# A fused block on one core: GpSimd instead of ScalarE begins eight of the first sixteen strip transfers of the attention

## The chip, the cores and the metric

The kernel runs on one core of one Trainium2 chip. The metric is the device time of one launch in microseconds (us). Times of single instructions come from one profiled execution. Engines: TensorE (PE; PEld is its weight load), VectorE (DVE), ScalarE (ACT), GpSimd (POOL) and SyncE (SP). ACTq and SPq are the issues of transfers in those engines' queues.

## The reference

`x` has 8 x 512 tokens of width 128, all in fp32.

```
x = x + 0.5 * ffn(layernorm(x))
x = x + attention(layernorm(x))     # one head, 4096 fixed memory keys and values
x = x + 0.5 * ffn(layernorm(x))

ffn:        sigmoid gate, the best 2 of 8 experts of 176 hidden units (bf16, squared relu),
            plus a shared expert in fp32
attention:  q = h @ Wq.T + bq;  p = softmax(q @ keys.T / sqrt(128));  (p @ values) @ Wo.T + bo
```

## The kernel before, in words

The tokens are 8 groups of 512 (4 tiles of 128). The first FFN runs over the groups up to about 118 us, the attention to about 560 us, the second FFN behind it. Each engine runs a fixed order written out by hand; semaphores connect them.

The attention has 16 **units** (u): a group of queries against one half (2048) of the keys. A unit has 8 **half steps** (h): tile i = h // 2 of the four, half h % 2 of its keys. In a half step TensorE computes the scores of 128 queries and 1024 keys (`scores`, six matmuls of 512 columns, L1311 to L1313, an fp32 product in three parts), VectorE takes their maximum (`maximum`, L1061; after the second half `neg_max`, L1067), and ScalarE the exponentials (`exponentials`, L726 or L736).

The product with the values needs the exponentials transposed, keys on the partitions. For some tiles of a unit this is done by VectorE, which transposes squares of 32 x 32 (`transpose_squares`, L1056), and by transfers that bring whole strips of squares from partitions i*32 to partitions b*32, from the tile `E2` to the tile `probsT` (`move_strip`, L331). There are 4 x 4 strips (b, i). In unit 0 two tiles (0 and 1) go this way, and tiles 2 and 3 ("own" tiles) are transposed by TensorE (`transpose_pair`, L1331); in the middle units it is three and one. In unit 0 each strip transfer is 32 partitions by two rows of 2 KB, 128 KB in all. They begin when the transposed squares of tiles 0 and 1 are there (`squares_done`); SyncE begins b = 0 and 1, eight transfers, ScalarE b = 2 and 3, eight transfers. In later units SyncE begins all but a few.

The strips are then used in pairs of key chunks, eight pairs (`ring`) to a unit: `moved_high` (ScalarE, L708) rounds the moved part, `moved_low` (GpSimd, L513) takes the rest; `own_high` (ScalarE, L700) and `own_low` (VectorE, L1049) do the same for the part that TensorE transposed; `values` (TensorE, L1352 to L1354) multiplies. In unit 0 the pairs begin early: ScalarE does moved_high(0) in half step 6, own_high(0) and moved_high(1) in half step 7; TensorE does transpose_pair(0) at half step 8, transpose_pair(1) at 9 and values(0) at 10. transpose_pair(1) waits for own_low(0) (`p_lo_done`), since both use the same PSUM bank. Scores use three pairs of banks in turn: a score block waits for the exponential three blocks before it.

The first `moved_high` of a unit waits for all sixteen strips of that unit:

```
if ring % UP == 0:
    for k in range(len(BATCHES)):
        wait(act, moved[k], moves(k, ring // UP + 1))
```

The eight transfers of ScalarE stand in its order behind the second exponential of tile 2 (u = 0, h = 5) and ahead of the first exponential of tile 3 (h = 6). In unit 0 GpSimd has nothing to do between its last instruction of the first FFN and `moved_low(0)`.

Of the kernel before, what the change touches and what calls it, by code (L numbers as in the profile page):

```python
# [17 lines left out]
GROUPS = TILES // GT  # L18
# [6 lines left out]
SLOTS = PAIRS + 1  # L25
# [13 lines left out]
LAST = UNITS - 1  # L39
# [5 lines left out]
SQ = 32  # L45
QUADS = P // SQ
# [41 lines left out]
def macaron_kernel(nc: bass.Bass, x, wup, wdown, gate_w, expert_bias, shared_up, shared_down,  # L88
                   wq, bq, wo, bo, keys_values, out):
    with ExitStack() as ctx:  # L90
# [3 lines left out]
        def sem(name):  # L94
            return ctx.enter_context(nc.semaphore(name))
# [35 lines left out]
        E2 = sb("E2", [P, MOVED, QUADS, N], fp32)  # L131
# [96 lines left out]
        down_done = sem("down_done")  # L228
        yT_copied = sem("yT_copied")
        z_done = sem("z_done")  # L230
# [8 lines left out]
        probsT_done = sem("probsT_done")  # L239
        squares_done = sem("squares_done")  # L240
        moved = [sem(f"moved{k}") for k in range(len(BATCHES))]
        p_hi_done = sem("p_hi_done")
        p_lo_done = sem("p_lo_done")
        moved_hi_done = sem("moved_hi_done")
# [16 lines left out]
        def wait(eng, s, n):  # L261

            if not isinstance(n, int) or n > 0:
                eng.wait_ge(s, n)
# [50 lines left out]

        def moves(k, units):

            return 16 * QUADS * QUADS * (units if k == 0 else max(0, min(units, LAST) - 1))

        def squares_of(units):  # L320
            return 2 * sum(moved_tiles(w) for w in range(units))
# [1 line left out]
        def batch_of(i):  # L323
            return [k for k, (first, count) in enumerate(BATCHES) if first <= i < first + count][0]

        def move_strip(eng, u, k, b, i):

            first, count = BATCHES[k]
            target = probsT[b * SQ:(b + 1) * SQ, u % 2, :, :, :].rearrange(
                "p (t i) c q -> p i t (c q)", t=MOVED)[:, i, first:first + count, :]  # L330
            eng.dma_start(target, E2[i * SQ:(i + 1) * SQ, first:first + count, b, :]).then_inc(moved[k], 16)  # L331

        def pairs_until(H):

# [57 lines left out]
        def _(pool):  # L392
# [144 lines left out]
            for u in range(UNITS + 2):  # L537
                g = u // 2
                for h in range(HALVES):

                    ring = pair_at(u * HALVES + h + 4)
                    if ring is not None:
                        moved_low(ring)
                    if has_next_group(u, u % 4) and h == 0:
                        inverse_deviation(g + 1 + ATTENTION_LN)
                        normalize(g + 1 + ATTENTION_LN, g + 1)
                    if u < UNITS and u % 2 == 1 and h == 1:
                        add_bias(g)
                    if 2 <= u < LAST and h == ADD_HALF:
                        add_block(u - 2)  # L550
                    if u == LAST + 1 and h == 4:
                        add_block(LAST - 2)
                    if u == LAST - 1 and h == 1:
                        inverse_deviation(SECOND_LN)
                        normalize(SECOND_LN, 0)
                    if u == LAST - 1 and h == 5:
                        inverse_deviation(SECOND_LN + 1)
                    if u == LAST and h == 3:
                        normalize(SECOND_LN + 1, 1)
                    if u == LAST and h == 4:  # L560
                        inverse_deviation(SECOND_LN + 2)
                    if u == LAST + 1 and h == 4:
                        inverse_deviation(SECOND_LN + 3)
# [4 lines left out]
        def _(act):  # L568
# [133 lines left out]
            def moved_high(ring):  # L702

                if ring % UP == 0:
                    for k in range(len(BATCHES)):
                        wait(act, moved[k], moves(k, ring // UP + 1))
                wait(act, pv_done, 2 * (ring - HI_RING + 1))
                act.activation(moved_part(p_hi, ring), moved_pair(ring // UP, ring % UP), ACT.Copy  # L708
                               ).then_inc(moved_hi_done, 1)

            def exponentials(u, i, h):

                v = u % 4
                act.wait_ge(neg_max_done, u * GT + i + 1)
                source = score_pair(u, i, h)
                if u == 0 and i == 0 and h == 0:
                    act.wait_ge(shared_up_done, GROUPS)
                    act.wait_ge(up_done, GROUPS * SLOTS)
                    act.wait_ge(weighted, GROUPS * SLOTS)
                if i < MOVED and h == 0:  # L720
                    wait(act, moved[batch_of(i)], moves(batch_of(i), u))
                    if u == 1 and i == MOVED - 1:
                        act.wait_ge(kv_lo_done, KV)
                if i < moved_tiles(u):
                    strips = E2[:, i, :, :].rearrange("p b (c q) -> p c b q", q=SQ)
                    act.activation(  # L726
                        strips[:, 2 * h * QUADS:2 * (h + 1) * QUADS, :, :],
                        source.rearrange("p k (c b q) -> p (k c) b q", b=QUADS, q=SQ), ACT.Exp,
                        bias=neg_max[:, v, i:i + 1], accum_out=row_sum[:, v, i, h:h + 1]).then_inc(exp_done, 1)
                else:  # L730
                    if i == MOVED and h == 0:

                        wait(act, probsT_done, UP if u == 1 else (u - 1) * UP)
                        if u < 2:
                            act.wait_ge(ffn_w_cast, 2)
                    act.activation(  # L736
                        own_exponentials(u, i)[:, 2 * h * N:2 * (h + 1) * N],
                        source.rearrange("p b n -> p (b n)"), ACT.Exp,
                        bias=neg_max[:, v, i:i + 1], accum_out=row_sum[:, v, i, h:h + 1]).then_inc(exp_done, 1)
# [23 lines left out]
            for u in range(UNITS + 2):  # L763
                g = u // 2
                prepares = u % 2 == 1 and u < LAST
                for h in range(HALVES):
                    H = u * HALVES + h
                    w = projection_at(H + 3)
                    if w is not None:
                        copy_oT(w)  # L770
                    if u == LAST + 2 and h == LAG - 2:
                        copy_oT(LAST)
                    if u == LAST + 1 and h == 3:
                        early_copy(1, banks[:, 1, :])
                    if u == LAST + 1 and h == 5:
                        exp_logits(GROUPS + 1, early_logits(1))
                        early_copy(2, banks[:, 0, :])
                    if u == LAST + 1 and h == 7:
                        exp_logits(GROUPS + 2, early_logits(2))
                    if u == LAST + 2 and h == 3:  # L780
                        copy_wbc(GROUPS, banks[:, 2, :])

                    ring = pair_at(H + 3)
                    if ring is not None:
                        own_high(ring)
                    if u < UNITS:
                        exponentials(u, h // 2, h % 2)
                    if u == 0 and h == 5:
                        act.wait_ge(z_done, GROUPS)
                        act.wait_ge(down_done, GROUPS * SLOTS)  # L790
                        act.wait_ge(squares_done, squares_of(1))
                        for b in range(QUADS // 2, QUADS):
                            for i in range(QUADS):
                                move_strip(act, 0, 0, b, i)
                    if 0 < u < LAST and h == HALVES - 1:
                        wait(act, moved_lo_done, UP * (u - 1))
                        act.wait_ge(squares_done, squares_of(u) + 2 * MOVED)
                        for i in range(QUADS):
                            move_strip(act, u, 1, QUADS - 1, i)
                    if prepares and h == Q_HALF - 2:  # L800
                        copy_xT_for_q(g + 1, TB)
                    if prepares and h == Q_HALF - 1:
                        q_high(g + 1, TB)
                    if u == LAST and h == Q_HALF - 2:
                        early_copy(0, TB)
                    if u == LAST and h == Q_HALF - 1:
                        exp_logits(GROUPS, early_logits(0))
                    ring = pair_at(H + 4)
                    if ring is not None:
                        moved_high(ring)  # L810
                    w = projection_at(H + 2)
                    if w is not None:
                        copy_y(w)
                    if 2 <= u and u % 2 == 0 and h == 1:
                        shift_exponentials(g - 1)
# [668 lines left out]
```

## Time and profile before

| | us |
|---|---|
| median of 3 runs | 663.71 |
| lowest, highest | 662.4, 664.31 |
| the profiled execution, its time | 662.44 |
| its span, first to last instruction | 660.8 |
| TensorE busy in the span | 614.2 |
| VectorE, ScalarE, GpSimd busy | 524.5, 461.3, 390.0 |
| mean granted clock of TensorE | 0.984 of full |

All times of rows are us from the span's start. The span is 1.64 us shorter than the execution's own time. An engine's busy time counts its instructions, not its waits and not the issuing of transfers.

### The profile page before, as it was taken

To read this page: it belongs to the slowest core of one execution; us is meant where nothing else is said; L and a number is where in the kernel's file an instruction comes from. 1 tells how busy PE (TensorE), PEld (TensorE's weight loads), DVE (VectorE), ACT (ScalarE), POOL (GpSimd) and SP (SyncE) were. 2 spreads that over 40 slices of the span, in tenths; PEclk is the share of its full clock that TensorE was granted. 3 is DMA by queue.
4 is the path that set the end of the run, shared out by engine and by line. 5 is a ranking of instruction groups with operands and counts; after the bars stand their busy time and mean duration, and the time that the engine had idled before them with its cause. 6 is when DMAs were issued, how large, how long until landed. Compare 5 with 4: busy or idle time off the path is not lost.

```text
span 660.8 us, 9207 instructions
## 1 busy us (share of the span) xinstructions
PE 614.2 (93%) x2800; PEld 429.1 (65%) x2800; DVE 524.5 (79%) x943; ACT 461.3 (70%) x765; POOL 390.0 (59%) x427
## 2 busy tenths in 40 slices
PE   3899999669899999999999999999999988999997
PEld 2555434447677877777778777777777867645442
DVE  4788877758978888887797897887898957698785
ACT  3567888446668767777776777777776774668886
POOL 3876970025366867767687587696677786524000
PEclk9799999979999999999999999999999998999999
DMA  8012020052573553744735627437355350000000
GB/s 301 1 33 65 32 64 0 2 126 65 128 160 87 137 132 76 172 95 101 160 84 141 135 64 176 107 93 163 90 131 116 84 121 1 0 18 17 32 33 32
DMA packets 35555, 59.06 MB, mean 89 GB/s; under 512 B 8539, under 2 KB 9139, under 8 KB 35379
## 3 DMA queue, kind: packets, MB, share of 16 engines
q1 hardware_dynamic: 31891, 53.75, 33.4%
q10 hardware_dynamic: 3616, 4.73, 2.8%
q8 instruction: 23, 0.38, 0.3%
q14 instruction: 25, 0.20, 0.1%
HBM read 8.12 MB, written 2.10 MB: 15 GB/s over the span
## 4 chain that ended last, share of the span: by engine, by line
PE 67%; DVE 18%; issue 5%; ACT 5%; SPq 1%; POOL 1%; ACTq 1%; DMA 1%; DVEq 0%; POOLq 0%
PE banks L1311 7%; PE banks L1352 7%; PE banks L1353 7%; PE banks L1354 7%; PE banks L1313 7%; PE banks L1312 7%; PE banks L1331 5%; DVE bank_max L1061 4%; DVE E L1056 4%; PE banks L1195 4%; PE banks L1186 3%; PE banks L1202 3%; PE banks L1149 3%; DVE probsT L958 3%; PE banks L1362 2%
## 5 line engine op out<-in xcount | busy, mean ns | idle before, releaser
L513 POOL TENSOR_TENSOR p_lo<-probsT,p_hi 128x768 fp32r<-128x768 f32 (+1 forms) x128 | 226.8, 1775 | 161.9 <-ACT p_hi L708 161.1
L1061 DVE TENSOR_REDUCE bank_max<-banks 128x1 f32<-128x1024 f32 x128 | 156.1, 1220 | 34.8 <-PE banks L1313 33.7
L708 ACT ACTIVATE p_hi<-probsT 128x768 fp32r<-128x768 f32 (+1 forms) x128 | 104.5, 816 | 28.0 <-PE banks L1354 24.0
L1311 PE MATMUL banks<-kv_lo,q_parts 128*128 128x512 f32 x256 | 112.0, 437 | 6.9 <-ACT E L726 4.4
L958 DVE SCALAR_TENSOR_TENSOR probsT<-banks,E 128x1024 bf16<-128x1024 f32 x80 | 95.5, 1218 | 28.7 <-PE banks L1186 28.1
L1056 DVE STREAM_TRANSPOSE E<-E 128x1024 f32<-128x1024 f32 x92 | 113.5, 1234 | 1.7 <-ACT E L726 1.7
L726 ACT ACTIVATE E<-banks,neg_max 128x1024 f32<-128x1024 f32 x92 | 102.3, 1113 | 8.5 <-DVE neg_max L1067 5.3
L1352 PE MATMUL banks<-p_hi,kv_lo 128*128 128x512 f32 x256 | 108.1, 422 | 0.0
L615 ACT ACTIVATE probsT<-probsT 128x1024 bf16<-128x1024 bf16 x96 | 91.8, 981 | 18.7 <-DVE probsT L958 15.5
L1353 PE MATMUL banks<-p_lo,kv_hi 128*128 128x512 f32 x256 | 102.8, 401 | 0.0
L1354 PE MATMUL banks<-p_hi,kv_hi 128*128 128x512 f32 x256 | 102.6, 401 | 0.0
L1313 PE MATMUL banks<-kv_hi,q_parts 128*128 128x512 f32 x256 | 101.6, 397 | 0.0
L1312 PE MATMUL banks<-kv_hi,q_parts 128*128 128x512 f32 x256 | 101.5, 397 | 0.0
L700 ACT ACTIVATE p_hi<-banks 128x256 fp32r<-128x256 f32 (+1 forms) x128 | 52.3, 408 | 63.1 <-PE banks L1331 62.9
L1049 DVE TENSOR_TENSOR p_lo<-banks,p_hi 128x256 fp32r<-128x256 f32 (+1 forms) x128 | 56.1, 438 | 43.1 <-ACT p_hi L700 42.6
L1331 PE MATMUL banks<-ident,probs 128*128 128x128 f32 x272 | 53.5, 280 | 10.7 <-ACT probs L736 6.6
L1311 PEld LDWEIGHTS banks<-kv_lo,q_parts 128*128 128x128 f32 x256 | 48.6, 190 | 15.3 <-ACT E L726 5.8
L1331 PEld LDWEIGHTS banks<-ident,probs 128*128 128x128 f32 x272 | 36.9, 143 | 32.9 <-ACT probs L736 7.0
L1354 PEld LDWEIGHTS banks<-p_hi,kv_hi 128*128 128x128 f32 x256 | 48.4, 189 | 12.4
L1352 PEld LDWEIGHTS banks<-p_hi,kv_lo 128*128 128x128 f32 x256 | 48.5, 190 | 11.8 <-issue 1.7
L1353 PEld LDWEIGHTS banks<-p_lo,kv_hi 128*128 128x128 f32 x256 | 48.5, 190 | 11.7 <-issue 1.7
L1186 PE MATMUL banks<-E,wup_b 128*128 128x512 bf16 x176 | 53.6, 392 | 2.4 <-DVE q_parts L1018 1.1
(118 smaller groups left out, 886.3 us busy)
## 6 DMA issues: line engine op xcount, KB each, us to landing
probsT<-E SPq DMA_DIRECT2D x248, 128.0 KB, 2.4
probsT<-E SPq DMA_DIRECT2D x168, 64.0 KB, 2.0
E<-in_keys_values SPq DMA_DIRECT2D x8, 512.0 KB, 3.5
probsT<-E ACTq DMA_DIRECT2D x56, 64.0 KB, 2.3
out<-X SPq DMA_DIRECT2D x8, 256.0 KB, 2.0
X<-in_x SPq DMA_DIRECT2D x1, 1280.0 KB, 8.9
probsT<-E ACTq DMA_DIRECT2D x8, 128.0 KB, 4.1
X<-in_x SPq DMA_DIRECT2D x3, 256.0 KB, 5.1
```

What stands on the lines that cost most here:

```text
L513: pool.tensor_tensor(moved_part(p_lo, ring), moved_pair(ring // UP, ring % UP), moved_part(p_hi, ring).bitcast(fp32), ALU.subtract).then_i ...
L708: act.activation(moved_part(p_hi, ring), moved_pair(ring // UP, ring % UP), ACT.Copy).then_inc(moved_hi_done, 1)
L958: dve.scalar_tensor_tensor(hidden[:, k, :, :], up_banks[PAIR_BANK[k]], 0.0, spread.unsqueeze(1).to_broadcast([P, 2, N]), ALU.max, ALU.mult ...
L1056: dve.transpose(half, half).then_inc(squares_done, 1)
L1061: dve.tensor_reduce(bank_max[:, i % 2, h:h + 1], score_pair(u, i, h).rearrange("p b n -> p (b n)"), AX.X, ALU.max).then_inc(bank_max_done, 1)
L1311: pe.matmul(bank, qh, kl, start=True, stop=False)
L1312: pe.matmul(bank, ql, kh, start=False, stop=False)
L1313: pe.matmul(bank, qh, kh, start=False, stop=True).then_inc(scores_done, 1)
L1331: last = pe.transpose(TB[:, at_column:at_column + P], own_exponentials(w, t)[:, c * P:(c + 1) * P], ident[:, :])
L1352: pe.matmul(OB, vl, hi, start=(c == 0), stop=False)
L1353: pe.matmul(OB, vh, lo, start=False, stop=False)
L1354: pe.matmul(OB, vh, hi, start=False, stop=(c == KC - 1)).then_inc(pv_done, 1)
```

## The change

The eight transfers of unit 0 that ScalarE began (b = 2 and 3) are begun by GpSimd, at the same half step of its own order, behind the same waits. Each gets a semaphore of its own (`moved_first`) in place of the common one, so the common count of unit 0 is eight transfers instead of sixteen (`moves`). ScalarE waits for the eight new semaphores ahead of moved_high(0), and again ahead of the first exponential of tiles 0 and 1 of unit 1, which overwrite the source.

```diff
+        moved_first = [sem(f"moved_first{k}") for k in range(QUADS * QUADS // 2)]
...
         def moves(k, units):
-            return 16 * QUADS * QUADS * (units if k == 0 else max(0, min(units, LAST) - 1))
+            if k == 0:
+                return 16 * QUADS * QUADS * units - (8 * QUADS * QUADS if units else 0)
+            return 16 * QUADS * QUADS * max(0, min(units, LAST) - 1)
...
-        def move_strip(eng, u, k, b, i):
+        def move_strip(eng, u, k, b, i, done=None):
...
-            eng.dma_start(target, E2[i * SQ:(i + 1) * SQ, first:first + count, b, :]).then_inc(moved[k], 16)
+            eng.dma_start(target, E2[i * SQ:(i + 1) * SQ, first:first + count, b, :]).then_inc(done or moved[k], 16)
...
             for u in range(UNITS + 2):            # GpSimd's order
                 g = u // 2
                 for h in range(HALVES):
+                    if u == 0 and h == 5:
+                        pool.wait_ge(z_done, GROUPS)
+                        pool.wait_ge(down_done, GROUPS * SLOTS)
+                        pool.wait_ge(squares_done, squares_of(1))
+                        for b in range(QUADS // 2, QUADS):
+                            for i in range(QUADS):
+                                move_strip(pool, 0, 0, b, i, moved_first[(b - QUADS // 2) * QUADS + i])
...
                 if ring % UP == 0:                # ScalarE, moved_high
                     for k in range(len(BATCHES)):
                         wait(act, moved[k], moves(k, ring // UP + 1))
+                if ring == 0:
+                    for done in moved_first:
+                        act.wait_ge(done, 16)
...
+                if u == 1 and i < 2 and h == 0:   # ScalarE, exponentials
+                    for done in moved_first:
+                        act.wait_ge(done, 16)
...
-                    if u == 0 and h == 5:         # ScalarE's order
-                        act.wait_ge(z_done, GROUPS)
-                        act.wait_ge(down_done, GROUPS * SLOTS)
-                        act.wait_ge(squares_done, squares_of(1))
-                        for b in range(QUADS // 2, QUADS):
-                            for i in range(QUADS):
-                                move_strip(act, 0, 0, b, i)
```

## Rows read from the trace of the kernel before

**Rows 1.** The page, engines' busy time; then the windows view of the attention.

```profile
PE 614.2 (93%) x2800; PEld 429.1 (65%) x2800; DVE 524.5 (79%) x943; ACT 461.3 (70%) x765; POOL 390.0 (59%) x427
...
144.75:540.00 395.25, 386.16 (x1821) 302.31 (x1819) 327.98 (x533) 289.38 (x526) 279.40 (x217) 1.00 0.51 118
```

**Rows 2.** The chain that ended last, 128 to 146 us: start, us, what.

```profile
130.72 0.75 ACTq L331
...
137.86 1.20 ACTq L331
...
139.10 0.02 ACTq L735
...
139.16 1.21 ACT probs L736 x2
```

**Rows 3.** The timeline of ScalarE: start, us, instruction, idle before and its releaser.

```profile
142.07 0.63 ACT L708 ACTIVATE p_hi<-probsT 128x512 fp32r<-128x512 f32 x1 [1.70 <-DMA probsT<-E]
...
143.08 1.10 ACT L736 ACTIVATE probs<-banks,neg_max 128x1024 f32<-128x1024 f32 x1
```

**Rows 4.** The timeline of VectorE.

```profile
133.71 0.15 DVE L1067 TENSOR_REDUCE neg_max<-bank_max 128x1 f32<-128x2 f32 x1
...
143.21 0.69 DVE L1049 TENSOR_TENSOR p_lo<-banks,p_hi 128x512 fp32r<-128x512 f32 x1 [6.93 <-ACT p_hi L700]
144.14 1.22 DVE L1061 TENSOR_REDUCE bank_max<-banks 128x1 f32<-128x1024 f32 x1 [0.23 <-PE banks L1313]
```

**Rows 5.** The timeline of TensorE.

```profile
140.42 1.12 PE L1331 MATMUL banks<-ident,probs 128*128 128x128 f32 x4 [6.60 <-ACT probs L736]
...
141.77 0.63 PE L1312 MATMUL banks<-kv_hi,q_parts 128*128 128x512 f32 x1
142.19 0.63 PE L1313 MATMUL banks<-kv_hi,q_parts 128*128 128x512 f32 x1
...
143.96 1.01 PE L1331 MATMUL banks<-ident,probs 128*128 128x128 f32 x4
...
146.44 0.40 PE L1353 MATMUL banks<-p_lo,kv_hi 128*128 128x512 f32 x1
146.68 0.40 PE L1354 MATMUL banks<-p_hi,kv_hi 128*128 128x512 f32 x1
...
550.78 0.38 PE L1331 MATMUL banks<-ident,E 128*128 128x128 f32 x1 [1.90 <-DVE p_lo L1049]
```

**Rows 6.** Windows: busy PE, PEld, DVE, ACT, POOL; granted clock, DMA share, GB/s.

```profile
25.28:35.52 10.24, 9.49 (x29) 5.95 (x30) 6.55 (x11) 5.95 (x9) 9.63 (x21) 0.50 0.01 2
550.78:554.34 3.56, 3.56 (x11) 2.98 (x12) 3.42 (x7) 0.91 (x2) 3.48 (x5) 0.52 0.00 0
137.92:140.42 2.50, 0.00 (x0) 0.00 (x0) 0.00 (x0) 1.21 (x2) 0.00 (x0) 0.50 0.89 243
140.42:144.74 4.32, 4.32 (x15) 3.36 (x15) 1.29 (x2) 2.67 (x5) 1.28 (x1) 0.50 0.14 37
132.10:141.60 9.50, 2.90 (x13) 2.23 (x12) 3.75 (x12) 1.21 (x2) 0.00 (x0) 0.81 0.89 221
160.00:167.40 7.40, 7.25 (x33) 5.33 (x33) 6.35 (x9) 4.50 (x10) 2.57 (x2) 1.00 0.92 203
```

**Rows 7.** The strip transfers (L331), issue ns min/median/max; units 0 and 1.

```profile
L331 ACTq DMA_DIRECT2D probsT<-E x8: 750/1026/1200, 130.7 to 137.9; - x8
...
DMA to landing us min/median/max: 2.6/4.0/4.4
...
L331 SPq DMA_DIRECT2D probsT<-E x14: 585/597/607, 158.7 to 167.1; - x14
...
DMA to landing us min/median/max: 2.4/2.4/2.5
```

**Rows 8.** The timeline of GpSimd.

```profile
142.77 1.28 POOL L513 TENSOR_TENSOR p_lo<-probsT,p_hi 128x512 fp32r<-128x512 f32 x1 [43.43 <-ACT p_hi L708]
...
179.53 1.84 POOL L513 TENSOR_TENSOR p_lo<-probsT,p_hi 128x768 fp32r<-128x768 f32 x1 [5.64 <-ACT p_hi L708]
```

## The prediction

> **What bounds the kernel now.** I read the page first. TensorE is busy 614.2 of 660.8 us, and over the long attention stretch from 144.75 to 540 us it is busy 386.16 of 395.25 us at full clock [rows 1]. So after 144 us there is next to no slack behind which lost TensorE time could hide: what delays TensorE there delays the end by the same amount.
>
> The chain of work that ended last, read between 128 and 146 us, goes through ScalarE's transfer issues from 130.72 to 139.06 us, then an exponential, and reaches TensorE at 140.42 us [rows 2]. Taken alone that looks like 8.3 us that could be had. But a chain follows only the last releaser at each step. So I read ScalarE's own timeline: after the issues it does the exponential of tile 3, first half (139.16), and then stops again, 1.70 us, until the transfers have landed, and does the first moved_high at 142.07 [rows 3]. moved_high(0) needs all sixteen transfers, SyncE's eight and ScalarE's eight. The question is therefore not when ScalarE is free, but when the last of the sixteen has landed. I call that time T; it is 142.07 us now.
>
> **Who waits for what around T.** ScalarE's order in the code is: exponential of tile 3 first half, moved_high(0), own_high(0), exponential of tile 3 second half. The three behind the first follow T directly, the last of them at 143.08 [rows 3]. VectorE's p_lo (own_low) follows own_high(0), at 143.21, and ends at 143.90; TensorE's transpose_pair(1) waits for it and starts at 143.96 [rows 4, 5]. From there TensorE has work without a break. None of these steps is shortened by the change. So TensorE's restart after the head is T + 1.89 before and after.
>
> **Part 1, ScalarE no longer issues: nothing on the path.** The maximum of tile 3 is there at 133.86 (133.71 + 0.15) [rows 4]. With the eight issues gone, the exponential starts at about 133.9 instead of 139.16, and TensorE, which follows its start by 1.26 us (139.16 to 140.42) [rows 2], does transpose_pair(0) and the next six score matmuls from 135.2 to 137.1: some 0.5 us for the transposes and 6 x 0.24 = 1.4 us by the distance of starts at full clock (146.44 to 146.68) [rows 5]. Then it stands until T + 1.89. What is gained is work that lies 5.3 us earlier and that nobody waits for: before, the same matmuls ended just when transpose_pair(1) became ready anyway. VectorE's maximum of those scores stands behind own_low in its order, so it moves only from 144.14 to 143.9 [rows 4]. The stall moves from before the exponential to behind it. Gain: 0.
>
> **Part 2, when the transfers land.** While the sixteen transfers run, the DMA engines are busy 0.89 of the time at 221 GB/s over 9.5 us, 2.1 MB [rows 6]; ScalarE's issues take 1.03 us each where SyncE's issues of the next unit, alone, take 0.60 us at every one, and landing takes 4.0 us where it then takes 2.4 (medians) [rows 7]. Two queues together carry hardly more than SyncE alone (221 against 203 GB/s) [rows 6], so the issues are held up by the engines, not the engines by the issues. GpSimd in ScalarE's place pushes the same bytes through the same engines. No row shows a transfer issued by GpSimd. Bounds for its issue, p, from the nearest rows: below, SyncE's alone, 0.64 us from start to start (fourteen starts from 158.7 to 167.1), which gives T = 130.72 + 8 x 0.64 + 1.8 (2.4 to landing less the issue) = 137.6; above, an ordinary GpSimd instruction, 1.84 us [rows 8], which gives 130.72 + 8 x 1.84 + 1.8 = 147.3. I take p where the same transfers now have it, 1.03 us [rows 7], so T stays at 142.07; shift 0, bounds -4.4 and +5.2. GpSimd itself has stood idle for 43.43 us when it comes to its first p_lo at 142.77 [rows 8]; behind the new wait and the eight issues (done by 139 at p = 1.03) stands only that p_lo, which waits for moved_high(0) in any case, so the cover holds until p is 1.4.
>
> The Trainium skill speaks here against a gain: "DMA: Bandwidth & Descriptors", "Rules for kernel authors", says that spreading transfers over issuing engines saves only issue time since the same engines move them. The rates of rows 6 agree. Its "Latency and other measured facts" gives the GpSimd path a first byte after about 1 us against 0.6 us; by that T would be an estimated 0.4 us later and the sum 0.4 us longer.
>
> **Part 3, TensorE's clock: a cost.** Before, TensorE stood for 6.60 us up to 140.42 [rows 5]. The granted clock was 0.50 from 137.92 on, 1.2 instead of 2.4 GHz, and stayed there until 144.74, 4.32 us after TensorE had resumed [rows 6]. But those 4.32 us mostly lay *ahead of* 143.96, where TensorE was waiting for T anyway; only 0.78 us of it fell on bound work. After the change TensorE stands from 137.1 to 143.96, 6.9 us, so the same dip comes, but TensorE resumes straight into bound work. By the starts of successive score matmuls (141.77 to 142.19, 0.42 us, against 0.24) [rows 5] each us at half clock loses 1 - 0.24 / 0.42 = 0.43 us. Cost: (4.32 - 0.78) x 0.43 = 1.5 us. Bounds: another dip lasted 3.56 us after TensorE resumed behind a gap of 1.90 us, the first of the run 10.24 us [rows 5, 6]: 10.24 gives (10.24 - 0.78) x 0.43 = 4.1 us. Below, no dip at all: -0.3 us, a gain of what it costs now (0.78 x 0.43). I take 1.5, since the gap is as long as the one that was followed by 4.32.
>
> **Part 4, the waits.** ScalarE gets eight more waits ahead of moved_high(0), and sixteen in unit 1. A wait of its queue shows as 0.02 us, and 0.04 us lie between it and the exponential behind it (139.10 to 139.16) [rows 2]; eight are at most 0.5 us if all stand behind T, and nothing if the last transfer is the last one waited for. I take 0.1. Those of unit 1 lie beside TensorE's work: ScalarE has room there (289.38 of 395.25 us busy) [rows 1]. Their cost if that cover were gone: 1.0 us.
>
> **The sum** against the profiled execution: 0 + 0 + 1.5 + 0.1 = +1.6 us. Its span is 660.8 and its time 662.44, so 1.64 us lie around the span; after: 664.0. The median of the runs before is 663.71, 1.27 above that execution, so I predict 665.3 us. A measurement of this kernel can't tell a change within 0.3% (2.0 us) from none, and this one lies just inside.
>
> **Rivals.**
> *GpSimd's stream runs out of step and lands sooner (faster).* SyncE and ScalarE run through the same source rows in lockstep; SyncE alone makes 203 GB/s [rows 6], so two streams that do not meet could carry more than 221 together. With SyncE done by about 137 and GpSimd at p = 0.87, T = 130.72 + 7.0 + 1.8 = 139.5, 2.6 us early. The gap is then 4.3 us; if the clock holds, the sum is -2.6 - 0.3 + 0.1 = -2.8: 660.9 us. It decides from T below 140.3 with the clock kept, or below 138.5 without. Against it: the low clock at 550.78 came behind a gap of 1.90 us alone [rows 5, 6]. For it: the gap would be a third shorter than the one that is followed by 4.32 us of low clock now. Chance 0.19.
> *GpSimd's issue is the slow one (slower).* With p = 1.5, between the row I take and the row above, T = 130.72 + 12 + 1.8 = 144.5, +2.5 us, and with parts 3 and 4 +4.1: 667.8 us. It becomes slower than 0.3% from T = 142.4, p = 1.24. The same holds if only the first transfer starts late, by 0.3 us or more, since GpSimd has issued none before. Chance 0.28. The Trainium skill ("GPSIMD Engine Reference", "Instruction dispatch") puts about 6 us on the first call of freshly loaded GpSimd code; if the transfer code were such a case the estimate would be 671.4. No row here shows whether it is.
> *The ScalarE stall was the bound after all.* If moved_high(0) were ready as soon as ScalarE is, the whole 5.3 us would come off: 658.4. Against it stands the 1.70 us wait for the transfers behind the exponential [rows 3]; I give it 0.03, which is in the faster chance of 0.20.
> *Nothing moves.* T stays and the dip is shorter or placed so that it costs under 1 us: 663.7 to 664.7. Chance 0.10.
>
> **How the numbers follow.** The forecast holds 0.40: T within 1 us of now and a dip of about 4 us behind the restart, +0.6 to +2.6 around 665.3; its own range is 664.3 to 666.3, and it splits 0.26 within 0.3% and 0.14 slower. With the rivals: faster 0.20 (both faster rivals, less 0.02 for a late T that keeps the clock), within 0.3% 0.38, slower 0.42. Range: below, the faster rival's 660.9; above, T of the slow rival with a longer dip (p = 1.6, T = 145.3, +3.2 + 2.6 + 0.1 = 5.9): 669.6. The ends p = 0.64 and 1.84 lie outside.
>
> **What would show it.** Right: ScalarE's exponential of tile 3 starts near 133.9; its moved_high(0) still near 142, now behind a wait of some 7 us for a transfer; TensorE has six score matmuls before 137.2 and a gap of nearly 7 us to about 144; the clock is 0.50 for some 4 us behind it, and transposes and scores there are 0.42 us apart. Wrong: T earlier than 140.3 or later than 143; GpSimd issues far from 1.03 us apart; the clock at 1.00 behind the gap.

## The result, and the profile after

The changed kernel takes 665.18 us (median of 20 runs, 662.37 to 668.69), the kernel before 663.57 us (20 runs, 660.48 to 665.49). The ratio is 1.0037, 95% interval 1.0023 to 1.0051: slower by 0.37%, clear of no change. A second series, with its own runs of the kernel before, gave 1.0021 (1.0004 to 1.0037). The recorded ratio is not the quotient of the two medians: these are 1.6 us apart in both series, 0.24% and 0.25%. The profiled execution took 665.67 us, its span 664.0 us, 3.2 us over that of before. One execution of e11 took 1066.41 us at a mean granted clock of 0.689 and is left out of its median and its ratio in the table.

First the issues of the strip transfers of unit 0 in the changed kernel: count, issue in ns min/median/max, first and last start.

```profile
L334 SPq DMA_DIRECT2D probsT<-E x8: 588/933/1917, 130.1 to 138.1; - x8
L334 POOL DMA_DIRECT2D probsT<-E x8: 533/533/787, 130.7 to 134.7; - x8
...
  ACT p_hi L721: 6.9, 1
```

GpSimd begins its eight within 4.5 us, the first issue taking 0.79 us and the others 0.53 us each, faster than SyncE alone does it in the next unit [rows 7]. But now SyncE's last issues are stretched, up to 1.92 us, and the last line says that ScalarE's moved_high waited 6.9 us for the transfers. The chain that ended last, and the packets from 139.7 to 142 us by queue, say for whose transfers it waited:

```profile
136.16 1.92 SPq L334
138.08 0.04 issue
138.12 3.28 DMA probsT<-E
141.40 0.02 issue
141.42 0.63 ACT p_hi L721
```

```profile
q1 hardware_dynamic: 126, 0.19, 31.5%
```

SyncE's last transfer is begun at 138.12 and lands at 141.40; in the last stretch SyncE's queue (q1) alone moves packets. GpSimd's eight transfers are through by then, so T is now set by SyncE's stream. The timeline of ScalarE shows where the stall has gone:

```profile
133.29 1.11 ACT L752 ACTIVATE probs<-banks,neg_max 128x1024 f32<-128x1024 f32 x1 [2.12 <-DVE neg_max L1076]
134.30 0.19 ACT L752 ACTIVATION_READ_ACCUMULATOR probs<-banks,neg_max 128x1 f32 x1
141.42 0.63 ACT L721 ACTIVATE p_hi<-probsT 128x512 fp32r<-128x512 f32 x1 [6.93 <-DMA probsT<-E]
...
142.43 1.11 ACT L752 ACTIVATE probs<-banks,neg_max 128x1024 f32<-128x1024 f32 x1
```

The exponential of tile 3 starts at 133.29 instead of 139.16, and the moved_high behind it at 141.42. The head of this execution ran 0.63 us earlier up to the first issue (130.08 instead of 130.71), so against the first issue T is 11.34 us, where it was 11.36 [rows 2, 3]. TensorE:

```profile
134.55 0.66 PE L1340 MATMUL banks<-ident,probs 128*128 128x128 f32 x4 [1.35 <-ACT probs L752]
134.96 0.48 PE L1320 MATMUL banks<-kv_lo,q_parts 128*128 128x512 f32 x1
...
136.21 0.40 PE L1322 MATMUL banks<-kv_hi,q_parts 128*128 128x512 f32 x1
143.32 1.11 PE L1340 MATMUL banks<-ident,probs 128*128 128x128 f32 x4 [6.71 <-DVE p_lo L1058]
...
145.93 0.63 PE L1321 MATMUL banks<-kv_hi,q_parts 128*128 128x512 f32 x1
146.36 0.63 PE L1322 MATMUL banks<-kv_hi,q_parts 128*128 128x512 f32 x1
...
147.94 0.40 PE L1362 MATMUL banks<-p_lo,kv_hi 128*128 128x512 f32 x1
148.18 0.40 PE L1363 MATMUL banks<-p_hi,kv_hi 128*128 128x512 f32 x1
148.42 0.60 PE L1340 MATMUL banks<-ident,probs 128*128 128x128 f32 x4
```

transpose_pair(0) and the six score matmuls lie early, then comes a gap of 6.71 us, and transpose_pair(1) starts at 143.32, T + 1.90. From there to transpose_pair(2) (148.42) it takes 5.10 us. In the first trace of before it took 3.66 us, from 143.96 [rows 5] to this line:

```profile
147.62 0.60 PE L1331 MATMUL banks<-ident,probs 128*128 128x128 f32 x4
```

The matmuls between start 0.43 us apart up to 147 and 0.24 us behind that. The windows say why (columns as in [rows 6]):

```profile
131.30:140.80 9.50, 3.96 (x19) 2.63 (x17) 3.74 (x12) 1.21 (x2) 3.91 (x8) 0.98 0.89 222
136.60:140.41 3.81, 0.00 (x1) 0.00 (x0) 0.00 (x0) 0.00 (x0) 0.00 (x0) 1.00 0.94 272
140.41:143.32 2.91, 0.00 (x1) 0.01 (x1) 0.75 (x2) 1.90 (x3) 1.19 (x1) 0.50 0.04 9
143.32:147.24 3.92, 3.92 (x12) 3.24 (x13) 2.13 (x4) 3.04 (x7) 1.84 (x3) 0.50 0.00 0
147.24:151.60 4.36, 4.36 (x22) 3.54 (x21) 4.00 (x4) 2.21 (x4) 4.14 (x9) 1.00 0.00 0
```

The transfers move at 222 GB/s, as before (221). The granted clock falls to 0.50 within the gap and stays there for 3.92 us after TensorE has restarted; in all that time TensorE is busy. So of the 3.2 us between the two spans, 1.44 us (5.10 - 3.66) arise here. The head gives 0.63 back. Of the other 2.4 us nearly all, 2.2 us, arise around 199 us: there TensorE stands 2.22 us instead of 1.38, at a wait for the strips of unit 1, and a stretch at half clock follows. The traces below show both kernels with such a stretch and without, so it can't be counted for the change.

### The profile page after: what moved, and what is told of

Its sections match the earlier page's. It is cut to its first block, busy times and chain, and to the rows that moved or that the text cites. A ratio compares the mean times of both kernels' runs of the same rounds, so it can differ in the third digit from the quotient of the medians.

```text
span 664.0 us, 9219 instructions
## 1 busy us (share of the span) xinstructions
PE 615.4 (93%) x2800; PEld 429.8 (65%) x2800; DVE 524.3 (79%) x943; ACT 461.0 (69%) x765; POOL 394.8 (59%) x435
## 3 DMA queue, kind: packets, MB, share of 16 engines
q0 software_dynamic: 384, 1.05, 0.6%
## 4 chain that ended last, share of the span: by engine, by line
PE 63%; DVE 17%; issue 5%; SPq 5%; ACT 5%; POOL 2%; DMA 2%; DVEq 0%; ACTq 0%; POOLq 0%
PE banks L1320 7%; PE banks L1322 7%; PE banks L1321 7%; PE banks L1361 7%; PE banks L1362 7%; PE banks L1363 7%; SPq L334 5%; PE banks L1340 4%; PE banks L1204 4%; PE banks L1195 3%; PE banks L1211 3%; DVE E L1065 3%; DVE bank_max L1070 3%; PE banks L1158 3%; DVE probsT L967 3%
## 5 line engine op out<-in xcount | busy, mean ns | idle before, releaser
L1322 PEld LDWEIGHTS banks<-kv_hi,q_parts 128*128 128x128 f32 x256 | 48.6, 190 | 11.6
```

The source lines that it names most:

```text
L1322: pe.matmul(bank, qh, kh, start=False, stop=True).then_inc(scores_done, 1)
```

## The experiments

T, the start of moved_high(0), is given against the first strip issue, which takes out what the head does from execution to execution. "Pair 1 to 2" is the time from the start of transpose_pair(1) to that of transpose_pair(2), all TensorE-bound work. "Gap" is TensorE's stand near 198 us, and "dip" whether the granted clock falls to 0.50 behind it. Each row's first three values come from one trace; the ratio is to runs of the kernel before made beside it.

| kernel | T, us | pair 1 to 2, us | gap, us; dip | median, us | ratio, 95% interval |
|---|---|---|---|---|---|
| before | 11.36 | 3.66 | 1.38; no | 663.57 | |
| e5, before | 11.33 | 4.29 | 1.45; no | 662.83 (one run) | |
| e12, before | 11.43 | 4.29 | 1.77; yes | 664.32 (one run) | |
| changed | 11.34 | 5.10 | 2.22; yes | 665.18 | 1.0037 (1.0023 to 1.0051) |
| e6, changed | 11.52 | 5.09 | 1.46; no | 664.86 | 1.0021 (1.0004 to 1.0037) |
| e9, fewer waits | 11.81 | 4.96 | 1.87; yes | 664.16 | 1.0027 (1.0007 to 1.0047) |
| e1, filled | 11.71 | 3.33 | 1.95; yes | 664.54 | 1.0036 (1.0018 to 1.0054) |
| e7, filled | 11.76 | 3.33 | 2.47; yes | 664.16 | 1.0009 (0.9995 to 1.0024) |
| e2, SyncE all | 12.14 | 4.85 | 2.18; yes | 666.21 | 1.0058 (1.0042 to 1.0073) |
| e3, changed, order | 10.65 | 5.45 | 2.42; no | 664.51 | 1.0023 (1.0003 to 1.0044) |
| e11, e3 filled | 10.68 | 3.31 | 1.83; no | 663.94 | 1.0029 (1.0005 to 1.0052) |
| e4, before, order | 10.05 | 3.31 | 1.95; no | 661.23 | 0.9978 (0.9960 to 0.9995) |
| e10, the same | 10.27 | 3.31 | 2.29; yes | 660.31 | 0.9970 (0.9947 to 0.9993) |
| e8, e4 filled | 10.09 | 3.33 | 1.94; yes | 663.52 | 0.9989 (0.9966 to 1.0012) |

**e1 and e7: is it the clock?** The changed kernel, and on TensorE, in the gap:

```diff
+                        if ring == 1:
+                            for _ in range(24):
+                                pe.matmul(OB, kv_hi[:, 0, 0:P], q_hi[:, 0, :], start=True, stop=True)
                         transpose_pair(ring)
```

> The changed kernel, with 24 matmuls of 512 columns that nobody reads put on TensorE (into the empty output bank) ahead of transpose_pair(1), where it stands for 6.7 us; 24 x 0.234 = 5.6 us, so they end before T + 1.89. Clock theory: the granted clock stays 1.00 behind the gap, the transposes and scores there run 0.24 us apart, transpose_pair(2) follows transpose_pair(1) by 3.7 us instead of 5.1, and the time falls by 1.4 to 1.8 us against the changed kernel, to about that of the kernel before (0.997 to 1.001 of it). Rival, the loss comes from GpSimd's path or from the waits and not from the clock: the time stays 1.5 to 2.5 us above the kernel before (1.002 to 1.004).

TensorE in e1:

```profile
136.51 5.77 PE L1449 MATMUL banks<-q_parts,kv_hi 128*128 128x512 f32 x24
143.77 0.66 PE L1340 MATMUL banks<-ident,probs 128*128 128x128 f32 x4 [1.48 <-DVE p_lo L1058]
...
146.86 0.40 PE L1363 MATMUL banks<-p_hi,kv_hi 128*128 128x512 f32 x1
147.09 0.60 PE L1340 MATMUL banks<-ident,probs 128*128 128x128 f32 x4
```

and its window of the restart:

```profile
143.50:147.00 3.50, 3.23 (x16) 2.71 (x17) 3.31 (x5) 3.29 (x7) 1.77 (x3) 1.00 0.00 0
```

At the place itself the theory holds: with TensorE kept busy the clock stays 1.00 and pair 1 to 2 takes 3.33 us instead of 5.10. The median did not follow; at 1.0036 it lay where the changed kernel's had been, which is what the rival had foretold for the time. So both kernels were measured again, side by side.

> The changed kernel once more, on the same chip as its neighbours here, for a second trace and a ratio taken beside theirs. Expected: 1.002 to 1.005 of before; T 11.3 us behind the first issue within 0.3; 4.7 to 5.5 us from transpose_pair(1) to (2), where before has 3.7; around 198 us either outcome.

> The kernel with the 24 filling matmuls once more, beside the changed kernel on one chip. Its first trace had the dip in the head gone and 3.33 us from transpose_pair(1) to (2) instead of 5.10, but its median came out as the changed kernel's (1.0036). If the clock's 1.5 us was real and the first median was scatter: 0.997 to 0.999 of e6. If the filling costs what it saves (T later: it was 11.73 us behind the first issue instead of 11.35): within 0.1% of e6, and T above 11.6 again.

The changed kernel came at 1.0021, the filled one at 1.0009. That is 0.12% or 0.8 us in the direction and the range of the clock theory, but the intervals overlap. T was 11.76 us, above the 11.6 of the other reading, but e9 has 11.81 without any filling, so that is no sure cost of it. The clock's cost is shown in the traces, in the medians only suggested. The granted clock of every execution is on record, not only that of the profiled ones. Its mean is 0.987 over 82 executions of the kernel before, 0.986 over 32 of the changed one and 0.990 over 20 of the filled one (e1, e7). So the change does not lower the clock by more than before did; it moves the low stretch onto work that nothing hides. And the filling does raise the clock in the runs without a trace too, yet little of that comes back as time.

**e2: does it need GpSimd?** The kernel before; SyncE issues all strips of unit 0, ScalarE's block is taken out.

```diff
-                    for b in range(QUADS // 2 if u == 0 else QUADS - k):
+                    for b in range(QUADS - k):
...
-                    if u == 0 and h == 5:
-                        ...
-                                move_strip(act, 0, 0, b, i)
```

> The kernel before with all sixteen strip transfers of unit 0 begun by SyncE and none by ScalarE; GpSimd issues nothing, no wait is added. Clock theory: ScalarE is free early, as in the change, T comes from SyncE's issues alone, 16 x 0.64 + 1.8 us behind the first, 12.0 instead of 11.4 us, so +0.7 us, and the dip behind the restart costs its 1.5 us again: +2.2 us against before (1.003). Rival, it is GpSimd that costs: only +0.7 us (1.001).

Its issues and what they lead to:

```profile
L331 SPq DMA_DIRECT2D probsT<-E x16: 587/597/736, 130.7 to 140.4; - x16
...
  ACT p_hi L708: 7.7, 1
...
DMA to landing us min/median/max: 2.4/2.4/2.5
```

T came out at 12.14 us (12.0 expected), TensorE stood 7.51 us, and pair 1 to 2 took 4.85 us, though GpSimd issues nothing and no wait is added. So the loss behind the restart belongs to the early start of ScalarE and not to GpSimd. Against e5 and e12 that is +0.8 us of T and +0.6 us behind it, 1.4 us; against the first trace of before 2.0. The ratio is 1.0058, 3.8 us: more than either theory gave, and the larger of the two (+2.2) is the nearer. What the rest is stays open; the mean granted clock of all six executions is low, 0.981 to 0.983, so some of it may be low clock at other places.

**e3 and e4: what sets T?** Only the order of the source strips in one of the two streams:

```diff
                         for b in range(QUADS // 2, QUADS):
-                            for i in range(QUADS):
+                            for i in (2, 3, 0, 1):
                                 move_strip(pool, 0, 0, b, i, ...)     # e3; in e4 the same for ScalarE's
```

> The changed kernel with GpSimd's eight transfers in the order of source i = 2, 3, 0, 1 in place of 0, 1, 2, 3, so that SyncE and GpSimd read other partitions at the same time. If the rate of 221 GB/s is one of partitions met by both streams: more than 260 GB/s, T 1.5 to 3.5 us earlier against the first issue (11.3 us now), and the time 1.5 to 4 us below the changed kernel. If the rate is that of the sixteen DMA engines whatever they read: T within 0.4 us and the time within 0.1% of the changed kernel.

> The kernel before with ScalarE's eight transfers in the order of source i = 2, 3, 0, 1, one edit. If the rate hangs on both streams meeting at the same partitions: T 1.5 to 3.5 us earlier against the first issue (11.4 us now), ScalarE's issues under 0.9 us each, and the time 1.5 to 4 us below before (0.994 to 0.998). If it is the engines' own rate: no change (0.999 to 1.001).

The issues of e4, and its transfers' window:

```profile
L331 SPq DMA_DIRECT2D probsT<-E x8: 587/603/1379, 128.6 to 134.1; - x8
L331 ACTq DMA_DIRECT2D probsT<-E x8: 617/807/1110, 128.7 to 134.3; - x8
```

```profile
130.00:138.00 8.00, 3.17 (x15) 2.31 (x14) 3.75 (x12) 1.21 (x2) 0.00 (x0) 0.94 0.96 262
```

```profile
136.59 0.73 PE L1331 MATMUL banks<-ident,probs 128*128 128x128 f32 x4 [4.83 <-ACT probs L736]
140.59 0.65 PE L1331 MATMUL banks<-ident,probs 128*128 128x128 f32 x4 [0.71 <-DVE p_lo L1049]
```

The same bytes by the same two queues go at 262 GB/s instead of 221, ScalarE's issue falls from 1.03 to 0.81 us (medians), T comes 1.3 us earlier (1.5 to 3.5 were expected), and TensorE's gap shrinks from 6.6 to 4.83 us. At 0.9978 it is faster than both the kernel before and the changed one. So the 221 GB/s was no rate of the sixteen engines whatever they read; it depended on both streams reading the same partitions in step. That is shown for the order. That the partitions' ports are what is met was not tried by itself. The Trainium skill ("SBUF — State Buffer", "Door 1: The DMA port swizzle") says that partitions 0 to 63 and 64 to 127 reach separate halves of the 16 DMA ports. That fits the order of e4, but no run here separates it from another cause. In e3 T moves by 0.7 us only, which neither branch of its expectation foretold. A likely reason, not tried, is that GpSimd begins its transfers 0.53 us apart and SyncE 0.60 us and more, so that the two soon fall out of the step that the order was made for. Its pair 1 to 2 is long again (5.45), and the ratio, 1.0023, lies between the two of the changed kernel, 1.0021 and 1.0037.

**e8, e10, e11: better versions.**

> A version meant to beat both: the kernel before with ScalarE's eight transfers in the order 2, 3, 0, 1, and 16 unread matmuls (3.7 us) on TensorE ahead of transpose_pair(0), in its gap of 4.8 us. Clock theory: no dip in the head, nothing lost behind transpose_pair(1), and 0 to 1 us below e4's 0.9978, so 0.996 to 0.998 of before. If filling costs by itself, as e1's median suggests: 0.998 to 1.000.

> The order 2, 3, 0, 1 for ScalarE's transfers in the kernel before, a second time, since it is the best so far (0.9978) and its version with filling matmuls came out unclear (0.9989). Expected: 0.996 to 0.999 of before, T 10.1 us behind the first issue.

> The changed kernel with both cures: GpSimd's transfers in the order 2, 3, 0, 1 and 24 filling matmuls. The traces so far give T 10.66 in place of 11.4 us (-0.7), 3.33 in place of 3.66 to 4.29 us from transpose_pair(1) to (2) (-0.3 to -1.0), and the filling's own delay of T (+0.3): -0.7 to -1.4 us, 0.998 to 0.999 of before. With 24 matmuls ending near T + 1.9 when T is early, up to 0.7 us of that may be lost, then 1.000.

e10 repeats e4: 0.9970. Whether filling adds anything to it can't be told (e8, 0.9989, 0.9966 to 1.0012), and at this place it had nothing to win: in e4 and e10 the low clock ended before transpose_pair(1), and pair 1 to 2 took 3.31 us without filling. e11 missed its expectation: its trace is as foretold, T 10.68 and 3.31 us behind the restart, and still its ratio is 1.0029. Two of the four filled series (e1, e11) lie clearly above what their first 150 us promise. What the filling costs elsewhere stays open, and the traces can't settle it. From transpose_pair(2) to the end of the span they take 513.2 us (before) to 517.4 us (e7), and e10, without any filling, takes 517.3. The best kernel is the one before with one list changed, not the changed one.

**e9: the waits.**

```diff
-                if u == 1 and i < 2 and h == 0:
-                    for done in moved_first:
-                        act.wait_ge(done, 16)
```

> The changed kernel without the sixteen waits in unit 1 (moved_high(0) has waited for the same eight transfers already). My term for all added waits was 0.1 us, with those of unit 1 hidden. Expected: within 0.1% of the changed kernel (1.0021 of before beside its neighbours), and the times from transpose_pair(1) to (2) and on to unit 2 as they were. Rival, the waits cost what they would without cover: 1.0 us or 0.15% less than the changed kernel.

1.0027 against the changed kernel's 1.0021 and 1.0037: nothing gained. The intervals (0.2% to each side) don't rule out the 0.15% of the rival, but the traces speak against it: from transpose_pair(2) to the first moved_high of unit 1, behind these waits, e9 took 31.45 us, and the changed kernel 31.38 and 31.56 us with them.

**e5 and e12: the place near 198 us.**

> The kernel before once more, for a second trace. In the first traces the changed kernel loses time at two places: 1.44 us between transpose_pair(1) and (2), and 2.4 us around 198 us, where ScalarE waits for the strips of unit 1 (TensorE stands 2.2 us instead of 1.4, and a dip of the clock follows). If the second place comes from the change: here TensorE stands 1.2 to 1.5 us again and no dip follows. If it is chance from execution to execution: 1.4 to 2.4 us, with or without a dip. The 3.66 us from transpose_pair(1) to (2) should come again within 0.4 us in either case.

> The kernel before a third time, for the two places that differ from execution to execution. Expected: T 11.3 to 11.5 us behind the first issue, 3.3 to 4.3 us from transpose_pair(1) to (2). If the place around 198 us is chance: TensorE stands between 1.4 and 2.5 us there, as it did in the other traces; if the change moved it: 1.4 us again, without a dip behind it.

e5 left the question open, since a gap of 1.45 us without a dip fits both readings. It missed at the other place: transpose_pair(1) to (2) took 4.29 us, where 3.66 within 0.4 was expected. e12 took 4.29 us as well. In these two traces the low clock lasted 10.24 us and ended 2.1 us behind the start of transpose_pair(1), where in the first trace of before it ended 0.78 us behind it.

e12, the kernel before, at the place near 198 us:

```profile
193.00:199.50 6.50, 4.73 (x23) 3.60 (x22) 3.15 (x5) 2.82 (x5) 3.57 (x3) 1.00 0.67 158
199.75:203.16 3.41, 3.41 (x10) 2.66 (x9) 2.51 (x5) 2.09 (x4) 3.08 (x2) 0.50 0.41 97
```

The dip of 3.41 us at half clock is there in the kernel before too, while e6, the changed kernel, has neither the long gap nor the dip. So the 2.2 us at this place in the first pair of traces must not be counted for the change. They are part of the scatter of single runs, some 5 us. Whether the change makes such a dip more likely, fourteen traces can't tell.

## Why the prediction was right

- **The chain's 8.3 us of issues are no gain: right.** ScalarE's exponential moved from 139.16 to 133.29 and T did not. The stall moved behind it, 6.93 us in place of 1.70.
- **T stays, since the rate and not the issue holds it: right in the size, half right in the reason.** T went from 11.33 to 11.43 us (three traces) to 11.34, 11.52 and 11.81, about +0.2 us. But I took p as 1.03 us with 0.64 as the lower bound; it is 0.53 behind the first issue, below the bound. With p = 0.53 my bound's formula gives T = 130.72 + 4.2 + 1.8 = 136.8, 5.3 us early. It did not happen, because SyncE's issues became slower as GpSimd's became faster (up to 1.92 us), and SyncE's last transfer set T. The transfers together hold T, at 222 GB/s against 221, and the formula, which had only one stream's issue in it, does not. Why SyncE's stream is the one held back was not tried; the same 1.05 MB went as 384 packets in GpSimd's queue and as 640 in SyncE's. "The same engines carry the same bytes" was too strong as a reason: e4 shows that their rate depends on the order.
- **The clock: right.** Gap 6.9 foretold, 6.71 measured; low clock behind the restart 4.32 foretold, 3.92 measured; 0.42 us from start to start against 0.43; cost +1.5 us against +1.44 in the first pair of traces. That this pair agrees so well is partly luck. I took the 0.78 us of low clock on bound work from one trace; it was 2.1 us in e5 and e12. Over all traces the cost is less, since before varies (3.66, 4.29, 4.29) where the change hardly does (5.10, 5.09, 4.96): +1.0 us on the mean. e2 has it without GpSimd, e1 and e7 lose it with the clock kept up.
- **The waits: right**, too small to see. Those of unit 1 gained nothing when they were taken out (e9). Those ahead of moved_high(0) cost nothing either: only 0.02 us lie between the last landing, at 141.40, and its start at 141.42, so the 0.2 us of T are not theirs.
- **The sum:** 1.6 us foretold. The places add up to 1.0 + 0.2 = 1.2 us; the two series measured 2.5 us (0.37%) and 1.4 us (0.21%) by their ratios and 1.6 us each by their medians. The 1.2 us rest on three traces of each kernel, and what the first series' ratio has above them is not accounted for. The median of 665.18 lies 0.1 us beside the predicted 665.3, which is partly luck: 665.3 was built on 663.71, and the twenty runs before gave 663.57. By the bound of 0.3% the first series is just on the slower side, where I had 0.42, against 0.38 for within it.
- **The rivals.** GpSimd's stream did run out of step with SyncE's, and in stretches the rate was higher (272 GB/s from 136.6 to 140.4), but the whole did not land sooner: SyncE had been held back. The slow GpSimd issue did not come. GpSimd's first issue did start late, 0.6 us behind SyncE's, which is more than the 0.3 us that I gave as enough for "slower". It cost nothing, since GpSimd's eight transfers were through before SyncE's. The 6 us that the Trainium skill ("GPSIMD Engine Reference", "Instruction dispatch") puts on freshly loaded code did not come either: the first issue took 0.79 us. (My 671.4 for that case should read 671.3, 665.3 + 6.) The rule of the Trainium skill ("DMA: Bandwidth & Descriptors", "Rules for kernel authors") that spreading transfers over issuing engines saves only issue time agrees with T, 11.34 to 11.81 us against 11.33 to 11.43.

## What to carry to other kernels

A chain of waits that runs through an engine's transfer issues does not say that the time would come free with them: look at the next instruction that needs the transfers' *landing*, and at which stream's last transfer it waits for. Work that is brought forward into the shade of a wait can cost: here TensorE then stood 6.7 us directly ahead of bound work and restarted it at half clock, where before it spent most of the slow stretch on work that had time. And where two queues move data between partitions at once, try the order in which they walk through them first; here one list was worth 0.2 to 0.3%, where moving the issues to another engine cost 0.2 to 0.4%.

## What the runs showed of the hardware that I had not expected

- GpSimd issues these transfers (32 partitions, two rows of 2 KB each) faster than SyncE or ScalarE: 0.53 us apart, at most 0.79 for the first, against 0.60 for SyncE undisturbed. Its issues were not stretched while the DMA engines were loaded (median 0.533 us); SyncE's were, to 1.92 us.
- SyncE's and ScalarE's queues, reading the same partitions in step, made 221 GB/s; with one of them two strips ahead, 262 GB/s.
- Filling TensorE's gap with unread matmuls kept the granted clock at 1.00 behind it in all four traces, and yet the medians of e1, e7 and e11 did not fall by as much as their traces gained there. Not explained.
- The same kernel has the clock low for 3.4 us at other places in other executions. Behind the gap near 198 us it was low in 8 of 14 traces, with gaps of 1.77 to 2.47 us; but gaps of 1.83, 1.95 and 2.42 us (e11, e4, e3) had no low clock behind them. One trace was 2.2 us longer there than another.
